# First W1 in two transfers, W2 right behind it, column tiles 8 ahead of W on SyncE's queue, and new orders for the first 15 steps

## The reference

```python
# layer 0: adapter with a layer norm; w1 is 512x128, w2 is 128x512
h = relu(x @ W1[id0] + b1[id0])
a = x + h @ W2[id0] + b2[id0]
normed = (a - mean(a)) * rsqrt(var(a) + 1e-5)
x = x + normed * gamma[id0] + beta[id0]
# layer 1: W is 512x512
x = x + x @ W[id1] + b[id1]
```

## Time and profile before

| what | value |
|---|---|
| median of 3 runs | 310.59 us (309.85, 310.81, 310.59) |
| the profiled execution's own time | 310.22 us |
| its span in the profile | 308.4 us |
| PE busy | 302.0 us, 98% of the span |
| DVE, ACT, POOL busy | 224.8, 212.4, 221.0 us |
| granted clock of PE | 1.00 in all 40 slices |
| moved by all transfers | 64.34 MB, 209 GB/s on average |

### The profile page before, as it was taken

One profiled execution on the slowest core, in us unless ns is written; L12 is line 12 of the kernel. 1 busy time (PEld: TensorE's weight loads), 2 busy tenths in 40 slices (PEclk: granted clock), 3 DMA queues, 4 the chain that ended last, 5 costly groups with the idle time before them and its releaser, 6 DMA issues.

```text
span 308.4 us, 4826 instructions
## 1 busy us (share of the span) xinstructions
PE 302.0 (98%) x1420; PEld 243.4 (79%) x1420; DVE 224.8 (73%) x642; ACT 212.4 (69%) x382; POOL 221.0 (72%) x181
## 2 busy tenths in 40 slices
PE   7899999999999999999999999999999999999995
PEld 6345778888888888888888888888888888888884
DVE  0099889578959869596987969688795968889610
ACT  0348687968887859686696858868596864867431
POOL 0068979969699995999779995999959994631000
PEclk9999999999999999999999999999999999999999
DMA  6997886398976896878766897667967381111122
GB/s 180 381 374 245 269 292 197 108 308 265 323 200 198 269 265 179 221 204 260 253 175 206 213 316 230 158 189 220 339 175 206 137 275 36 68 69 71 68 102 102
DMA packets 40399, 64.34 MB, mean 209 GB/s; under 512 B 6068, under 2 KB 10164, under 8 KB 40372
## 3 DMA queue, kind: packets, MB, share of 16 engines
q1 hardware_dynamic: 38976, 61.41, 63.8%
q10 hardware_dynamic: 1396, 2.62, 2.6%
HBM read 47.24 MB, written 16.78 MB: 208 GB/s over the span
## 4 chain that ended last, share of the span: by engine, by line
PE 94%; DMA 2%; DVE 1%; SPq 1%; issue 0%; ACT 0%
PE out_ps L899 56%; PE h_ps L899 14%; PE down_ps L899 14%; PE turn_ps L969 9%; DMA w<-w_all 2%; SPq L194 1%; DVE turn_ps L607 0%; SPq L222 0%; DVE x1T_lo L614 0%; ACT out_sb L430 0%; DVE y L563 0%; PE down_ps L934 0%; PE out_ps L934 0%; PE out_ps L969 0%; DVE rstd L592 0%
## 5 line engine op out<-in xcount | busy, mean ns | idle before, releaser
L899 PE MATMUL out_ps<-x1T_hi,w_hi 128*128 128x512 f32 x256 | 100.9, 394 | 0.0
L899 PE MATMUL out_ps<-x1T_lo,w_hi 128*128 128x512 f32 x256 | 99.8, 390 | 0.0
L899 PE MATMUL out_ps<-x1T_hi,w_lo 128*128 128x512 f32 x256 | 99.7, 389 | 0.0
L800 POOL TENSOR_TENSOR xrow<-xrow,b_rows 128x512 f32<-128x512 f32 x60 | 77.4, 1295 | 0.0
L421 ACT ACTIVATE x1T_hi<-turn_ps,gamma_beta 128x512 fp32r<-128x512 f32 x63 | 42.5, 690 | 37.7 <-DVE turn_ps L607 37.7
L607 DVE SCALAR_TENSOR_TENSOR turn_ps<-turn_ps,gamma_beta,xT 128x512 f32<-128x512 f32 x63 | 44.9, 753 | 31.8 <-PE turn_ps L969 31.1
L805 POOL TENSOR_TENSOR xT_lo<-xT,xT_hi 128x512 fp32r<-128x512 f32 x48 | 62.2, 1296 | 4.7 <-ACT xT_hi L364 4.7
L412 ACT ACTIVATE y<-y,shift,rstd 128x512 f32<-128x512 f32 x64 | 51.9, 817 | 18.6 <-DVE shift L598 18.0
L899 PEld LDWEIGHTS out_ps<-x1T_hi,w_hi 128*128 128x128 f32 x256 | 48.1, 188 | 10.4 <-issue 0.5
L899 PEld LDWEIGHTS out_ps<-x1T_hi,w_lo 128*128 128x128 f32 x256 | 48.1, 188 | 10.2 <-issue 0.5
L899 PEld LDWEIGHTS out_ps<-x1T_lo,w_hi 128*128 128x128 f32 x256 | 48.1, 188 | 10.0
(11 more groups left out here) (55 smaller groups left out, 363.1 us busy)
## 6 DMA issues: line engine op xcount, KB each, us to landing
out_cols<-out_sb SPq DMA_DIRECT2D x64, 256.0 KB, 2.9
xrow<-x_rows SPq DMA_DIRECT2D x29, 512.0 KB, 6.3
xT<-x_cols SPq DMA_DIRECT2D x28, 512.0 KB, 6.0
w<-w_all SPq DMA_DIRECT2D x8, 1024.0 KB, 7.2
w<-w_all SPq DMA_DIRECT2D x15, 256.0 KB, 5.1
b_rows<-b_all SPq DMA_DIRECT2D x8, 256.0 KB, 7.9
xT<-x_cols ACTq DMA_DIRECT2D x4, 256.0 KB, 4.3
xT<-x_cols ACTq DMA_DIRECT2D x2, 512.0 KB, 8.6
```

The lines of the kernel that those rows point to most:

```text
L800: nc.gpsimd.tensor_tensor(xrow[:, i % XR, :], xrow[:, i % XR, :], b2_rows[:, m % 2, :], ALU.add).then_inc(rowbias_done, 1)
L899: mm = nc.tensor.matmul(out, lhsT, rhs, start=first and n == 0, stop=last and n == len(terms) - 1, skip_group_check=unchecked)
```

## The change

The first W1 comes in two transfers of 128 KB where it was four of 64 KB, and `up(0)` to `up(3)` wait by pairs. The lists of the first 15 steps are put in another order on all five engines; a few `out(i)` are cut into their quarters, with other work between them. No computation is added or taken away.

```diff
-        w1_first_in = [sem(f"w1_first_in{k}") for k in range(KC)]
+        w1_first_in = [sem(f"w1_first_in{k}") for k in range(2)]
...
-                sp.dma_start(w1[:, 0, k], w1_all[ds(row + k * P, P), :]).then_inc(w1_first_in[k], 16)
+                sp.dma_start(w1[:, 0, k:k + 2], w1_all[ds(row + k * P, 2 * P), :]
+                             .rearrange("(c p) a -> p c a", p=P)).then_inc(w1_first_in[k // 2], 16)
...
             def opening():                      # SyncE
                 load_first_w1(0)
-                load_first_w1(1)
                 load_first_w1(2)
-                load_first_w1(3)
+                load_w2(0)
                 load_b1(0)
-                load_w2(0)
                 load_first_b2()
+                load_cols(sp, nc.sync, 8)
                 load_w(0)
-                load_cols(sp, nc.sync, 8)
                 load_w1(1)
-                load_gamma_beta(0)
                 load_b2(1)
-                load_w2(1)
+                load_b1(1)
                 load_cols(sp, nc.sync, 10)
...
                 load_ids()                      # ScalarE
-                load_rows(act, nc.scalar, 4)
                 load_cols(act, nc.scalar, 4)
                 load_cols(act, nc.scalar, 6)
+                load_rows(act, nc.scalar, 4)
                 relu(0)
+                w_high(0, 0)
                 standard(0)
                 standard(1)
-                w_high(0, 0)
+                w_high(0, 1)
                 relu(1)
-                w_high(0, 1)
                 standard(2)
...
                     if i < KC:
-                        pe.wait_ge(w1_first_in[k], 16)
+                        pe.wait_ge(w1_first_in[k // 2], 16)
...
                 seed(3)                         # TensorE
-                up(4)
                 down(0)
                 down(1)
                 down(2)
                 down(3)
+                up(4)
                 up(5)
```

More of the change, by code:

```diff
@@ L303, in opening @@
[L303 to L307, removed]
+                load_rows(sp, nc.sync, 16)
+                store(0)
+                load_cols(sp, nc.sync, 20)
+                store(1)
+                load_gamma_beta(2)
+                store(2)
+                load_rows(sp, nc.sync, 18)
+                load_b2(2)
+                store(3)
+                load_rows(sp, nc.sync, 20)
@@ L472, in opening @@
                 normalise(5)
-                x_hi(16)
+                w_high(1, 0)
+                x_hi(17)
                 normalise(6)
+                normalise(7)
+                x_hi(18)
                 standard(8)
[L476 to L480, removed]
+                w_high(1, 1)
                 relu(3)
-                x_hi(18)
+                load_table()
                 h_high(3)
@@ L485, in opening @@
                 standard(10)
+                x1_high(4)
+                x1_high(5)
+                finish(2)
+                x_hi(19)
                 standard(11)
                 x1_high(6)
-                x_hi(19)
+                x1_high(7)
+                w_high(1, 2)
+                x_hi(20)
+                finish(3)
                 normalise(8)
[L490 to L493, removed]
                 normalise(9)
-                w2_high(2)
+                standard(12)
                 normalise(10)
@@ L498, in opening @@
                 relu(4)
-                w_high(1, 2)
                 finish(4)
                 w_high(1, 3)
-                x_hi(20)
-                standard(12)
+                standard(13)
+                finish(5)
+                x1_high(8)
                 h_high(4)
-                x1_high(8)
-                finish(5)
-                standard(13)
                 x1_high(9)
@@ L663, in opening @@
                 add_rows(7)
+                rstd_start(4)
+                rstd_newton(4)
                 statistics(6)
[L665 removed]
+                rstd_end(4)
+                statistics(7)
+                rstd_start(5)
+                mean_shift(4)
                 mean_variance(6)
[L667 to L669 removed]
                 rstd_newton(5)
@@ L838, in opening @@
                 w_low(0, 0)
+                bias_rows(5)
                 w_low(0, 1)
-                bias_rows(5)
                 w_low(0, 2)
+                w_low(0, 3)
                 bias_rows(6)
                 bias_rows(7)
+                bias_rows(8)
                 w2_low(1)
-                w_low(0, 3)
-                bias_rows(8)
                 h_low(2)
+                w_diagonal(1)
                 bias_rows(9)
@@ L852, in opening @@
                 x_lo(16)
-                bias_rows(12)
-                w_diagonal(1)
                 x_lo(17)
@@ L870, in opening @@
                 x_lo(20)
+                h_low(4)
+                bias_rows(16)
+                bias_rows(17)
+                w2_low(2)
             def step(s):
@@ L1022, in opening @@
                 down(6)
+                up(12)
                 turn(2)
-                up(12)
+                turn(3)
+                out_part(0, 0)
                 up(13)
-                turn(3)
+                out_part(0, 1)
                 down(7)
-                out(0)
+                out_part(0, 2)
+                out_part(0, 3).then_inc(out_done, 1)
                 out(1)
+                out_part(2, 0)
+                out_part(2, 1)
                 down(8)
+                out_part(2, 2)
                 down(9)
-                out(2)
+                out_part(2, 3).then_inc(out_done, 1)
+                down(10)
+                down(11)
                 up(14)
                 turn(4)
+                up(15)
                 turn(5)
-                down(10)
                 out_part(3, 0)
-                up(15)
                 out_part(3, 1)
-                down(11)
-                turn(6)
+                up(16)
+                up(17)
                 out_part(3, 2)
                 out_part(3, 3).then_inc(out_done, 1)
+                out_part(4, 0)
+                out_part(4, 1)
+                turn(6)
                 turn(7)
-                up(16)
-                up(17)
                 down(12)
                 down(13)
-                out_part(4, 0)
-                out_part(4, 1)
                 up(18)
+                down(14)
+                up(19)
                 out_part(4, 2)
                 out_part(4, 3).then_inc(out_done, 1)
-                down(14)
-                out_part(5, 0)
-                up(19)
-                out_part(5, 1)
+                out(5)
                 turn(8)
                 turn(9)
-                out_part(5, 2)
-                out_part(5, 3).then_inc(out_done, 1)
                 out(6)
                 out_part(7, 0)
+                turn(10)
                 out_part(7, 1)
-                turn(10)
+                out_part(7, 2)
                 turn(11)
-                out_part(7, 2)
                 out_part(7, 3).then_inc(out_done, 1)
```

159 lines of the change are left out of this document (76 added, 83 removed).

## The result

The changed kernel takes **313.39 us** (median of 4 runs, 313.26 to 314.46) against 310.40 for the kernel before beside it (309.85 to 310.81): a ratio of 1.010, interval 1.0083 to 1.0118. It is slower by 3.0 us, where 1.9 were forecast over the execution profiled before (312.3 for the median, range 311.1 to 313.8). Ratios and intervals, here and in the table, leave out the few executions that took over 1.5% more than the fastest of their kernel; the medians are of all.

The account below looks back on a forecast made before the run. PE was taken as the bound, with the end following `down(4)`. 310.22 us + 1.88 (W's chain through ACT) + 0.05 = 312.15; with the median 0.37 higher giving 312.5, the forecast was 312.3, range 311.1 to 313.8.

Parts of the forecast that it names:

- the likeliest case: Whole kernel: 311.7 (W landing 0.6 us sooner) to 313.1 us (0.5 us of further waits), held at 0.62.
- the rest: Behind `down(4)`: new lists cost nearly nothing; 0 to 0.3 us of loss at `turn(0)`, taken as 0.05.
- W behind column tiles 8: Opening: W lands 1.37 us later, at 18.58; ACT's reordered list then delays `down(4)` by 1.88 us, to 23.37.
- the same other bytes ahead of W: Opening: W1, W2, b2 and ACT's queue ahead of W unchanged, so only column tiles 8's 524,288 bytes delay it.
- b1 behind W2: Opening: b1 lands at 12.7 (12.0 to 13.7), `down(0)` at 14.8; alone a loss of 1.2 us.
- they don't add: At `down(4)`: W's chain, at 23.37, hides b1's loss because PE's own arrival is earlier, at 22.7.
- both prices: W2's transfer ahead of b1: 0.68 us at full rate, 1.36 us if ACT's queue takes half.
- The path b1 + 2.09 + 7.94: PE's arrival at `down(4)`: 2.09 us from b1 to `down(0)`, then 7.94 of PE's work, reaching 22.7 us.
- W1 in two: Opening: `up(0)` at 8.8 for 7.57 us, second pair over by 14.1; no term in the sum.
- the rival "faster": Opening: two W1 transfers save 2.3 us, the filled idle quarter 0.6; `down(4)` 1.0 us sooner, 309.6 us; chance 0.07.
- No change: Rival: W lands over 1 us sooner than its bytes say, leaving PE's arrival; about 311.3 us; chance 0.13.
- The clock's rival: Before `up(0)` and `down(4)`: long PE waits lower the clock, costing 0.5 to 1.5 us; 313 to 314; chance 0.08.

Follow-up runs that it names:

- all fourteen profiles: Profiles of the kernel before, the changed kernel (twice) and eleven edited kernels; medians 309.55 to 315.16 us.
- three rows of the table: Changed kernel with W ahead of column tiles 8: alone 312.18 us; with ACT's list also back 312.52; with b1 also ahead of W2 311.22.
- the six edits of the kernel before: Kernel before with: W1 in two 309.55 us, plus tiles 4 first 309.89, or plus b1 between 310.93; tiles 8 first 310.66; ACT's new list 311.23; last two together 312.76.
- the one pair of profiles that has it apart: Changed kernel with ACT's list and W's place back, 312.52 us; the same with b1 also ahead of W2, 311.22 us.
- the two kernels with one edit undone: Changed kernel with ACT's list as before, 311.91 us; changed kernel with W ahead of column tiles 8 again, 312.18 us.
- the second profile: Changed kernel run again unchanged: median 313.24 us, profiled execution 313.87 us.
- undoing W's half: Changed kernel with W ahead of column tiles 8 on SP's queue again: 312.18 us, ratio 1.0055 to the kernel before.
- undoing both: Changed kernel with ACT's list as before and W ahead of column tiles 8 again: 312.52 us, ratio 1.0056 to the kernel before.
- ACT's list back: Changed kernel with `w_high(0, 0)` behind the two standards and `w_high(0, 1)` behind `relu(1)`, as before: 311.91 us, ratio 1.0048 to the kernel before.

## Why the prediction was right, point by point

The deciding chain was right and its starting point too early. The 313.39 us lie above the likeliest case (311.7 to 313.1). They are inside the range only because it was stretched towards 314 for long waits of PE and a falling clock, a case with a chance of 0.08 that is not what set the median: on that side the hit is the width of the range and not the sum.

**The bound, and the place to measure: right.** `down(4)` sets the end in all fourteen profiles. The term for "the rest" (0.05 us) held to 0.3 us: span less `down(4)` is 287.0 before and 287.3 and 287.1 after. The "0.2 us" of waiting at `down(0)` and again at `down(4)` were read too large: in the timelines the first of the four records there takes 0.70 us and the others 0.59, which is 0.1 each. Nothing in the sum hangs on it.

**W behind column tiles 8, and the chain behind it: mechanism right, size off.** The chain from W to `down(4)` was forecast at 4.79 us and measured at 4.86 in three kernels. The mis-sized term is "W lands at 18.58": it landed at 19.70 and 20.18, 2.5 and 3.0 us later than before and not 1.37. Edits in the kernel before show that the bytes were priced right (1.16 and 1.78). What came on top is the change's own opening. With W ahead of column tiles 8 again the changed kernel still had W at 17.93 to 18.37 (three rows of the table), 0.7 to 1.2 us later than before, where I had taken "the same other bytes ahead of W" for the same time. W's landing is marked by sixteen completions, one for each DMA engine, and the wait ends behind the last (19.55, and `w_diagonal(0)` at 19.70). By these completions the mean engine was through at 16.29 us before, at 16.34 in the changed kernel with W first and at 18.13 in the changed kernel; the last one at 17.06, 18.05 and 19.55. So the lag of the last engine behind the mean is 0.8 us before and 1.2 to 1.7 in the seven profiles of the changed kernel and its variants, with or without column tiles 8 ahead. In the six edits of the kernel before it is 0.6 to 1.8, so that it belongs to the change is likely and not shown. In the profiled execution of the changed kernel the DMA engines also moved less from 5 to 10 us, 173 and 308 GB/s for 191 and 365: 187 KB, or 0.5 us at 383 GB/s. Which edit makes one engine fall behind, and why, stays open.

**b1 behind W2: the path right, the landing and its bounds too early, and "they don't add" right.** b1 was forecast for 12.7, within 12.0 to 13.7. It landed at 14.06 and 14.49 in the changed kernel, and at 12.75 to 13.12 with one or both edits undone. W2's place ahead of it was worth 1.77 us in the one pair of profiles that has it apart (13.12 and 11.35), more than both prices, 0.68 and 1.36; two issues fewer were worth 1.7 and not 1.0 (12.32 to 10.60). The two errors go against each other, so that 12.7 was met in some executions is in part luck. The path b1 + 2.09 + 7.94 was met within 0.1 us in the two kernels with one edit undone. It was hidden as forecast in the second profile (`down(0)` at 16.53 and 7.91 are 24.44, for a `down(4)` of 25.04), which is why undoing W's half gave back 1.1 us only and undoing both no more than one: behind one path stood the other.

**W1 in two: nothing in the sum, and a gain alone.** I named 8.8 us for `up(0)`; it was 10.1 in the changed kernel and 7.5 to 8.6 in most of its variants. The gain that the rival "faster" rested on is there: 0.8 us in the kernel before and 1.8 in the changed one (0.7 by the one execution with a full clock), far from the 2.3 + 0.6 of that rival, and W did not land sooner by it (17.44 to 17.21). The Trainium skill (DMA: Bandwidth & Descriptors, "Rules for kernel authors") advises to coalesce many small transfers; the two runs agree in direction.

**The table load's drain: not there.** After, as before, the next instruction, where it waits for nothing else, starts 0.02 us behind the load (21.64 and 1.28, then a `std` at 22.94). The Trainium skill (ScalarE: Activation LUTs, "What ACT_TABLE_LOAD costs") has about 1380 ns of drain; with it the chain would have been 6.2 us and not 4.86.

**The rivals.** No change fell with W's landing: the DMA engines had no room. The clock's rival took place in some executions: both profiles of the changed kernel show the lower level behind a wait of 2.9 to 3.4 us for W1. But the three executions of 313.26 to 313.51 us had clocks of 0.999 to 1.000, so the median's excess over the forecast is not the clock. They were not profiled; worked out, 311.5 us of span less 287.2 puts their `down(4)` at 24.3, and W, 4.86 ahead of it, at 19.4, which fits the 19.33 with ACT's list back.

## What to carry to other kernels

Where an in-order engine's list is rewritten, ask for each wait that moves forward what work that ran in idle time (here a table load and two small roots) is now queued behind it, and sum it from the landing of what is waited for: that sum was right to 0.1 us. Write down all paths that meet at the deciding instruction, with their arrival times; undoing one edit pays only down to the next path, and edits that cost little apart (0.4 and 0.9 us) cost 2.5 together. Try the parts of a change that lost one by one: the coalescing of W1 inside it was worth 0.26% alone.

## What the runs showed that I had not expected

A transfer at the start of the program lands when the slowest of the sixteen DMA engines is through, and that varied by 3 us: the first half of W1 was complete at 10.0 us in both profiles of the changed kernel, where the mean engine was through at 7.1 and 7.4, at 10.7 in one other (7.8), and at 7.4 to 8.5 in the six other profiles of kernels with two halves. With ACT's list back, and the same lists up to there, it was 7.4, so it differs from execution to execution. Where it was late, PE idled for 2.9 us or more at 7 to 10 us, its granted clock fell to the lower level, and it stayed there through the first matmuls. The length of the wait alone doesn't tell: the clock fell behind waits of 1.84 and 2.37 us for `relu(0)` in two profiles and stayed at 1.00 through waits of 2.33 and 2.51 us in two others. An issue on SP's queue, mostly 0.3 to 0.9 us, held the queue 2.25 us (b2, from 5.23, at a DMA share of 0.60) and 2.63 us (the second b1, from 11.51, at 1.07) in the changed kernel; what held it is not shown.
